# First feed-forward planes through two PSUM banks by thirds, and a fourth bank for the front ring

## The chip, the cores and the metric

The kernel runs on one core of a Trainium2 chip. Its engines work side by side and meet only at semaphores: TensorE (PE, whose weight loads are shown as PEld), VectorE (DVE), ScalarE (ACT), GpSimd (POOL) and SyncE (SP), which issues the DMAs. The metric is the device time of one execution in microseconds.

## The reference

The input x is 8 x 96 x 128 x 128 in float32. Two layers run one after the other. In short:

```
# layer 0
x = x + cluster(ln_c(x))            # 1x1 convolutions, 4 heads, 2x2 folds, 4 centres per fold:
                                    # cosine similarity, sigmoid, hard assignment to the best centre,
                                    # gather to the centres and back, 1x1 projection
t = tokens(x)
t = t + ffn(ln_t(t))                # h = relu(qlin(x, W1, b1)); y = qlin(h, W2, b2); 96 -> 384 -> 96
# layer 1
x = x + conv(ln_c(x))               # depthwise 3x3, 1x5, 5x1, then 1x1, times the normalised input
t = t + ffn(ln_t(t))
```

`qlin` rounds both factors to an 8-bit float (5 exponent, 2 mantissa bits) and the sums to a 16-bit one.

## The kernel before, in words

Three phases run one after the other. Phase A is layer 0 (and the normalisation that opens layer 1), phase B is the depthwise convolutions, phase C is the rest of layer 1. The change touches phase A alone.

Phase A treats 32 quarters of 64 x 64 tokens. A quarter has 4096 tokens: 8 chunks of 512, each held as 4 blocks of 128 tokens by 96 channels. The work of a quarter is spread over five steps: in step i the kernel runs the feed-forward network of quarter i, the projection back of quarter i+1 ("out", added to the tokens by DVE, "x1"), the similarities of quarter i+2, the centres of quarter i+3, and the turn of quarter i+4 from channels to tokens ("fwd"). A step has 9 slots, s = 0 to 8. Every engine has its own list, written out by hand, of what it does in each slot; an engine never leaves its order. The tables `BIG_AT`, `OUT_AT`, `FWD_AT`, `C_AT_BEFORE` and so on say in which slot each piece stands.

The feed-forward network of chunk k is: PE turns the 8-bit tokens to channels (`pe_q8`, L258); ACT copies them from PSUM to `q8c` (L296); PE multiplies by W1, three matmuls of 128 x 512, into the tile `hid`, which fills three PSUM banks (L272); ACT copies all three thirds with one instruction, 128 x 1536, to `h` (L307); DVE adds the bias and takes the maximum with zero in three instructions (L229) and rounds to 8 bits in one (L233), giving `hq`; PE multiplies by W2 (`pe_y`, L288); ACT copies the result (`y`, L318); DVE adds it to the tokens (L240, L244). In slot s, PE turns chunk s+1, runs the W1 product of chunk s and the W2 product of chunk s-1.

PSUM has eight banks. Phase A gives three to `hid`, two to the "back" ring (`bbank`: q8, y, and the turned planes "c" that ACT takes out by L805) and three to the "front" ring (`fbank`: all other products). A ring gives its banks round robin in program order, 36 uses of the front ring a step. Before PE writes a use it waits until the use that held the bank last has been read out:

```
n = self.number[stage, k]
for _ in self.uses:
    n -= len(self.banks)
```

In slots 3 to 6 the front ring's uses are, in order: big 6, big 7, out 0, out 1, pool; out 2, out 3, cf; out 4, out 5, simT 0, cn2; out 6, out 7, fwd 0, fwd 1. "big" is the product L608, taken out by ACT (L776, L777) and reduced by DVE (L902). "out" is L691, taken out by DVE (L983). "cn2" and its like are the tiny products at L682. "pabd" is the projection matrix that DVE writes in slot 2 (L976).

Of the kernel before, what the change touches and what calls it, by code (L numbers as in the profile page):

```python
# [53 lines left out]
class Events:  # L54
# [132 lines left out]
class FeedForward:  # L187
# [121 lines left out]
    def act_y(self, act, i, k):  # L309
# [61 lines left out]
def phase_a(nc, consts, x, wf_t, wf, bf, wv_t, bv, wp_t, bp, alpha, beta, w1, b1, w2, b2, gamma, beta_ln, x2_dram, x3_dram):  # L371
# [4 lines left out]
    with ExitStack() as ctx:  # L376
# [3 lines left out]
        for s in range(FFN_SLOTS):  # L380
# [17 lines left out]
            if s == AGG_AT:  # L398
# [172 lines left out]
        def _(pe):  # L571
# [182 lines left out]
        def _(act):  # L754
# [53 lines left out]
            def body(i):  # L808
                q1, q2, q3, q4, p = i + 1, i + 2, i + 3, i + 4, i - 1
                for s in range(FFN_SLOTS):  # L810
                    if i.real and s + 1 < NK:
                        ff.act_q8(act, i, s + 1)
                    if i.real and s < NK:
                        ff.act_hidden(act, i, s)
                    for k in C_AT_BEFORE.get(s, ()):
                        if p.real:
                            c_out(p, k)
                    for c in BIG_AT.get(s, ()):
                        if q2.real:
                            big(q2, c)  # L820
                    if i.real and s >= 1:
# [981 lines left out]
```

## Time and profile before

| | us |
|---|---|
| median of 3 runs | 4256.6 (4250.14 to 4260.43) |
| the profiled execution | 4258.63 |
| its span | 4256.8 |
| phase A in it | about the first 2142 |
| PE, DVE, ACT busy in the whole span | 3309.3, 3027.4, 2686.4 |

The span runs from the first to the last instruction. A busy time is the time in which an engine had an instruction in work. Idle time of an engine costs something only where its next work is on the path that sets the end. L12 is line 12 of the kernel. "A <- B" in a row of waits says that A's engine stood idle until B was done.

### The profile page before, as it was taken

Reading aid. Unit: us, or ns where it says so; the run is one execution under the profiler, and the core shown is the slowest. Engines: PE = TensorE matmul, PEld = TensorE weight load, DVE = VectorE, ACT = ScalarE, POOL = GpSimd, SP = SyncE. Lnnn points to the kernel's source line nnn. Section 1 sums busy time; section 2 is a strip of 40 time slices with the busy share of each in tenths; the row PEclk is TensorE's granted clock in tenths of the full one; section 3 lists DMA queues with packets and bytes.
Section 4 is the critical chain, followed back from the end, with each engine's and each line's share of the span. In section 5 each row is a group of like instructions: output and inputs, shape, how many; then the busy total and the mean of one; then the engine's idle time right before and its main releaser. Section 6 shows DMA issues by size and latency. Waiting matters only on the chain. (4 is left out here: it accounts for less than half of the span.)

```text
span 4256.8 us, 81198 instructions
## 1 busy us (share of the span) xinstructions
PE 3309.3 (78%) x26660; PEld 2549.8 (60%) x26660; DVE 3027.4 (71%) x7852; ACT 2686.4 (63%) x5250; POOL 1408.0 (33%) x1892
## 2 busy tenths in 40 slices
PE   6767777676776777767669999999788777778787
PEld 5556555555555555555549999999544444444443
DVE  4888888888888888888842222222388788778787
ACT  2567667676676776766752222222388788888887
POOL 3555555555555555555310000000022221212221
PEclk8888788888888887888879999999799999999998
DMA  3133232332323323222146656656766565666562
GB/s 62 44 75 83 67 77 61 75 83 68 75 65 78 83 61 75 71 72 68 53 111 163 168 160 164 166 161 165 183 178 179 151 178 156 174 170 171 155 175 77
DMA packets 733857, 489.89 MB, mean 115 GB/s; under 512 B 420796, under 2 KB 712956, under 8 KB 721276
## 3 DMA queue, kind: packets, MB, share of 16 engines
q1 hardware_dynamic: 733564, 486.32, 43.3%
q8 instruction: 143, 2.34, 0.2%
q14 instruction: 150, 1.23, 0.1%
HBM read 284.42 MB, written 201.33 MB: 114 GB/s over the span
## 5 line engine op out<-in xcount | busy, mean ns | idle before, releaser
L1722 POOL TENSOR_SCALAR C_var<-C_st 128x16 f32<-128x16 f32 x64 | 13.2, 207 | 1775.8 <-DVE C_st L178 1775.8
L1264 PE MATMUL B_ps_row<-B_g,B_z 128*128 128x128 f32 x4608 | 555.8, 277 | 0.6 <-ACT B_g L1296 0.6
L1264 PEld LDWEIGHTS B_ps_row<-B_g,B_z 128*128 128x128 f32 x4608 | 532.2, 193 | 0.7 <-ACT B_g L1296 0.7
L178 DVE BATCH_NORM_STATS2 A_st<-A_xT 128x6 f32<-128x192 f32 x1536 | 446.7, 350 | 30.7 <-ACT A_xT L764 17.3
L166 POOL TENSOR_TENSOR A_rstd<-A_var,A_expo 128x16 f32<-128x16 f32 x128 | 454.2, 3549 | 23.8 <-POOL A_var L163 23.6
L1357 DVE TENSOR_TENSOR B_mid<-B_ps_row,B_row_bias 128x512 f32<-128x512 f32 x192 | 132.8, 692 | 457.7 <-PE B_ps_row L1264 447.7
L1394 ACT ACTIVATE C_q<-C_xT,C_shift,C_rstd 128x96 fp8e5<-128x96 f32 x1024 | 392.0, 457 | 41.5 <-POOL C_shift L1729 41.0
L307 ACT ACTIVATE A_h<-A_hid 128x1536 f16<-128x1536 f32 x256 | 370.6, 1448 | 55.4 <-PE A_hid L272 51.6
L307 ACT ACTIVATE C_h<-C_hid 128x1536 f16<-128x1536 f32 x256 | 370.5, 1447 | 20.0 <-PE C_hid L272 12.9
L794 ACT ACTIVATE A_xc<-A_xT,A_shift,A_rstd 128x96 f32<-128x96 f32 x1024 | 379.4, 462 | 0.0
L229 DVE TENSOR_SCALAR A_hq<-A_h,A_b 128x512 f16<-128x512 f16 x768 | 240.8, 369 | 178.9 <-ACT A_h L307 178.6
L608 PE MATMUL A_fbank<-A_big_w,A_xq 97*128 97x112 f32 x2048 | 305.4, 313 | 66.3 <-DVE A_pabd L976 64.6
L608 PEld LDWEIGHTS A_fbank<-A_big_w,A_xq 97*128 97x128 f32 x2048 | 297.0, 227 | 93.6 <-DVE A_pabd L976 79.4
L1308 ACT ACTIVATE B_y<-B_ps_col,B_col_bias 128x512 f32<-128x512 f32 x192 | 132.0, 687 | 318.2 <-PE B_ps_col L1275 318.2
L1577 PE MATMUL C_fbank<-C_y3q,C_pw 96*96 96x512 f32 x512 | 280.9, 632 | 48.6 <-DVE C_gated L1653 24.3
L229 DVE TENSOR_SCALAR C_hq<-C_h,C_b 128x512 f16<-128x512 f16 x768 | 224.6, 349 | 122.9 <-ACT C_h L307 80.5
L288 PE MATMUL A_bbank<-A_w,A_hq 128*128 128x96 f16 x3072 | 219.4, 234 | 98.7 <-ACT A_x3h L805 85.8
L288 PEld LDWEIGHTS A_bbank<-A_w,A_hq 128*128 128x128 f16 x3072 | 197.7, 115 | 145.5 <-issue 112.7
L296 ACT ACTIVATE A_q8c<-A_bbank 96x512 bf16<-96x512 f32 x256 | 150.8, 590 | 197.5 <-PE A_bbank L258 196.2
L691 PE MATMUL A_fbank<-A_pabd,A_simT 128*128 128x384 f32 x512 | 261.2, 646 | 5.2 <-DVE A_xT L983 4.3
L1436 ACT ACTIVATE C_y<-C_bbank 96x512 f16<-96x512 f32 x256 | 150.2, 587 | 160.7 <-PE C_bbank L1423 156.9
L1586 PEld LDWEIGHTS C_fbank<-C_cst,C_gated 96*128 96x128 f32 x1024 | 113.2, 145 | 220.7 <-issue 111.9
(162 smaller groups left out, 7778.4 us busy)
## 6 DMA issues: line engine op xcount, KB each, us to landing
A_xq<-in_x SPq DMA_DIRECT2D x32, 1536.0 KB, 8.9
x_scratch<-A_xT SPq DMA_DIRECT2D x64, 768.0 KB, 3.2
x_scratch<-A_x3h SPq DMA_DIRECT2D x64, 768.0 KB, 5.4
B_z<-x_scratch SPq DMA_DIRECT2D x96, 512.0 KB, 5.0
y_scratch<-B_y SPq DMA_DIRECT2D x96, 512.0 KB, 3.7
C_x3q<-x_scratch SPq DMA_DIRECT2D x32, 1536.0 KB, 9.2
C_y3q<-y_scratch SPq DMA_DIRECT2D x32, 1536.0 KB, 15.5
C_xT<-x_scratch SPq DMA_DIRECT2D x64, 768.0 KB, 14.7
```

The lines of the kernel that those rows point to most:

```text
L166: m = pool.tensor_tensor(rstd[:, o:o + n], var[:], expo[:, 0:n], ALU.pow)
L178: return dve.bn_stats(st[:, n:n + 2, :].rearrange("p t s -> p (t s)"), x[:, n * C:(n + 2) * C].rearrange("p (t c) -> p c t", t=2))
L229: r = dve.tensor_scalar(self.hq[:, b, s], self.h16[:, b, s], self.w["b1"][:, j:j + 1], 0.0, ALU.add, ALU.max)
L288: m = pe.matmul(bank[:, t * C:(t + 1) * C], self.hq[:, b, s:s + P], self.w["w2"][:, j, :], start=(j == 0), stop=(j == NJ - 1))
L296: act.activation(self.q8c[:, k % 2, :], self.ring.bank("q8", k)[0:C, 0:CH], ACT.Copy).then_inc(self.ev["q8c"], 1)
L307: act.activation(self.h16[:, k % 2, :], self.hid[:, :], ACT.Copy).then_inc(ev["h16"], 1)
L608: m = pe.matmul(bank[:, t * BIGN:(t + 1) * BIGN], xq[q.buf(NX)][:, n * P:(n + 1) * P], big_w[:, :], start=True, stop=True)
L691: pe.matmul(front.bank("out", k)[:, 0:CW], simT[q.buf(2)][:, k, :], pabd[:], start=True, stop=True).then_inc(ev["out_full"], 1)
L794: m = act.activation(xc3[:, k // 4, t % (NT // 2), :], xT[u.buf(NB)][:, t * C:(t + 1) * C], ACT.Identity, scale=rstd3[:, t:t + 1], bias=sh ...
L1264: m = pe.matmul(ps_row[h][:, b * P:(b + 1) * P], z[c.buf(NB)][:, h * HB + b, d:d + W], g[c.buf(2)][:, d, :], start=(d == 0), stop=(d == 2))
L1394: m = act.activation(self.q8[:, t, :], x[:, t * C:(t + 1) * C], ACT.Identity, scale=self.rstd[:, t:t + 1], bias=self.shift[:, t:t + 1], sa ...
L1577: pe.matmul(rows(front.bank("pw", k)[0:C, 0:CH]), pw[:], group(y3q[q.buf(2)], k), start=True, stop=True).then_inc(ev["pw_full"], 1)
```

## The change

The class of the feed-forward network gets a variant for phase A. `hid` becomes two tiles of one bank each, and the thirds n = 3k+j of all chunks alternate between them. Each third has its own matmul with its own semaphore step, its own ACT copy (three of 128 x 512 in place of one of 128 x 1536), and its own wait on DVE. PE writes third n when ACT has copied third n-2. The first two thirds of a chunk stay where all three stood; the last third is moved back: on PE and ACT behind the first "big" of the slot, or, in slots without a "big", behind the turned planes (and, on PE, behind the W2 product of the chunk before). The bank that `hid` gives up makes the front ring four banks long.

```diff
+        self.hid2 = [ctx.enter_context(nc.psum_tensor(phase + f"hid{p}", [P, CH], F32)) for p in range(2)]
...
+    def pe_hidden(self, pe, i, k, j):
+        ev, n = self.ev, NJ * k + j
+        if j == 0:
+            pe.wait_ge(ev["q8c"], ev.at("q8c", i, k))
+        if n >= 2:
+            pe.wait_ge(ev["h16"], ev.at("h16", i, n - 2))
...
+        pe.matmul(self.hid2[n % 2][:], self.w["w1"][:, j * P:(j + 1) * P], self.q8c[:, k % 2, :],
+                  start=True, stop=True).then_inc(ev["hidden"], 1)
+    def act_hidden(self, act, i, k, j):
...
+        act.activation(self.h16[:, k % 2, j * CH:(j + 1) * CH], self.hid2[n % 2][:], ACT.Copy).then_inc(ev["h16"], 1)
+    def dve_hidden(self, dve, i, k):
+        ev, b = self.ev, k % 2
+        for j in range(NJ):
+            s = slice(j * CH, (j + 1) * CH)
+            dve.wait_ge(ev["h16"], ev.at("h16", i, NJ * k + j))
+            r = dve.tensor_scalar(self.hq[:, b, s], self.h16[:, b, s], self.w["b1"][:, j:j + 1], 0.0, ALU.add, ALU.max)
...
-        front = Ring(front_uses, [ctx.enter_context(nc.psum_tensor(f"A_fbank{p}", [P, 512], F32)) for p in range(3)])
+        front = Ring(front_uses, [ctx.enter_context(nc.psum_tensor(f"A_fbank{p}", [P, 512], F32)) for p in range(4)])
...
-                        ff.pe_hidden(pe, i, s)
+                        ff.pe_hidden(pe, i, s, 0)
+                        ff.pe_hidden(pe, i, s, 1)
                     for k in C_AT_BEFORE.get(s, ()):
                         if p.real:
                             c_turn(i, p, k)
-                    for c in BIG_AT.get(s, ()):
-                        if q2.real:
-                            big(i, c)
-                    if i.real and s >= 1:
+                    bigs = BIG_AT.get(s, ()) if q2.real else ()
+                    for c in bigs[:1]:
+                        big(i, c)
+                    if i.real and s >= 1 and not bigs:
+                        ff.pe_y(pe, i, s - 1)
+                    if i.real and s < NK:
+                        ff.pe_hidden(pe, i, s, 2)
+                    for c in bigs[1:]:
+                        big(i, c)
+                    if i.real and s >= 1 and bigs:
                         ff.pe_y(pe, i, s - 1)
```

ACT's list is cut in the same way; there `y` stays last in every slot.

PE, end of slot 5 and start of slot 6 of a step in the middle of phase A, before. L691 is out 4 and 5, L620 simT 0, the tiny L682 cn2, L258 the turn of chunk 7, L272 the W1 product of chunk 6, L288 the W2 product of chunk 5.

```order
L691 MATMUL A_fbank<-A_pabd,A_simT 128x384 [waits A_x1] x2
L620 MATMUL A_fbank<-A_cst,A_sim 128x128 [waits A_cfc,A_sim]
L620 MATMUL A_fbank<-A_cst,A_sim 128x128 x3
L682 MATMUL A_fbank<-A_csq,A_cst 96x4 [waits A_x1,A_csq]
L258 MATMUL A_bbank<-A_idb,A_q 96x128 [waits A_norm2,A_cout]
L258 MATMUL A_bbank<-A_idb,A_q 96x128 x3
L272 MATMUL A_hid<-A_q8c,A_w 128x512 [waits A_h16,A_q8c]
L272 MATMUL A_hid<-A_q8c,A_w 128x512 x2
L288 MATMUL A_bbank<-A_w,A_hq 128x96 [waits A_y16,A_hq]
```

The same place now; L746 is out, L675 simT, L737 cn2, L348 a third of the W1 product.

```order
L746 MATMUL A_fbank<-A_pabd,A_simT 128x384 [waits A_pooled]
L746 MATMUL A_fbank<-A_pabd,A_simT 128x384 [waits A_x1]
L675 MATMUL A_fbank<-A_cst,A_sim 128x128 [waits A_x1,A_sim]
L675 MATMUL A_fbank<-A_cst,A_sim 128x128 x3
L737 MATMUL A_fbank<-A_csq,A_cst 96x4 [waits A_cfc,A_csq]
L258 MATMUL A_bbank<-A_idb,A_q 96x128 [waits A_norm2,A_cout]
L258 MATMUL A_bbank<-A_idb,A_q 96x128 x3
L348 MATMUL A_hid<-A_q8c,A_w 128x512 [waits A_h16,A_q8c]
L348 MATMUL A_hid<-A_q8c,A_w 128x512 [waits A_h16]
L288 MATMUL A_bbank<-A_w,A_hq 128x96 [waits A_y16,A_hq]
L288 MATMUL A_bbank<-A_w,A_hq 128x96 x11
L348 MATMUL A_hid<-A_q8c,A_w 128x512 [waits A_h16]
```

The order of the front ring is the same; what cn2 waits for has moved from an `x1` of DVE (out 4 read out) to `cfc` (cf read out, a slot earlier). The last third stands behind the W2 product.

PE, slot 3, before: the W1 product of chunk 3, big 6, big 7 and the W2 product of chunk 2.

```order
L272 MATMUL A_hid<-A_q8c,A_w 128x512 [waits A_h16,A_q8c]
L272 MATMUL A_hid<-A_q8c,A_w 128x512 x2
L608 MATMUL A_fbank<-A_big_w,A_xq 128x112 [waits A_pabd]
L608 MATMUL A_fbank<-A_big_w,A_xq 128x112 x3
L608 MATMUL A_fbank<-A_big_w,A_xq 128x112 [waits A_sided]
L608 MATMUL A_fbank<-A_big_w,A_xq 128x112 x3
L288 MATMUL A_bbank<-A_w,A_hq 128x96 [waits A_y16,A_hq]
```

The same place now; L663 is big.

```order
L348 MATMUL A_hid<-A_q8c,A_w 128x512 [waits A_h16,A_q8c]
L348 MATMUL A_hid<-A_q8c,A_w 128x512 [waits A_h16]
L663 MATMUL A_fbank<-A_big_w,A_xq 128x112 [waits A_big]
L663 MATMUL A_fbank<-A_big_w,A_xq 128x112 x3
L348 MATMUL A_hid<-A_q8c,A_w 128x512 [waits A_h16]
L663 MATMUL A_fbank<-A_big_w,A_xq 128x112 [waits A_pabd]
L663 MATMUL A_fbank<-A_big_w,A_xq 128x112 x3
L288 MATMUL A_bbank<-A_w,A_hq 128x96 [waits A_y16,A_hq]
```

The wait for `pabd` has moved from big 6 to big 7.

ACT, slot 4, before: q8c of chunk 5, h of chunk 4, two turned planes, y of chunk 3.

```order
L296 ACTIVATE A_q8c<-A_bbank 96x512 [waits A_q8_full]
L307 ACTIVATE A_h<-A_hid 128x1536 [waits A_relu,A_hidden]
L805 ACTIVATE A_x3h<-A_bbank,A_gb 96x512 [waits A_x3_st1,A_c_full]
L805 ACTIVATE A_x3h<-A_bbank,A_gb 96x512 [waits A_c_full]
L318 ACTIVATE A_y<-A_bbank 128x384 [waits A_yb,A_y_full]
```

The same place now; L361 is a third of h, L867 a turned plane.

```order
L296 ACTIVATE A_q8c<-A_bbank 96x512 [waits A_q8_full]
L361 ACTIVATE A_h<-A_hid 128x512 [waits A_relu,A_hidden]
L361 ACTIVATE A_h<-A_hid 128x512 [waits A_hidden]
L867 ACTIVATE A_x3h<-A_bbank,A_gb 96x512 [waits A_x3_st1,A_c_full]
L867 ACTIVATE A_x3h<-A_bbank,A_gb 96x512 [waits A_c_full]
L361 ACTIVATE A_h<-A_hid 128x512 [waits A_hidden]
L318 ACTIVATE A_y<-A_bbank 128x384 [waits A_yb,A_y_full]
```

The last third of h now follows the two turned planes.

## Rows read from the trace of the kernel before

**Rows 1.** Busy time by engine, of phase A and of the rest.

```profile
core 0: us, PE busy (x) PEld busy (x) DVE busy (x) ACT busy (x) POOL busy (x), PEclk, DMA share, GB/s
0.00:2142.00 2142.00, 1516.17 (x14228) 1197.86 (x14228) 1770.81 (x4819) 1434.73 (x2984) 1161.67 (x1624) 0.83 0.29 70
2142.00:4257.00 2115.00, 1793.16 (x12432) 1351.99 (x12432) 1256.60 (x3034) 1251.68 (x2267) 246.35 (x268) 0.95 0.59 161
```

**Rows 2.** Who waited for whom, 300 to 1900 us: total, times, longest.

```profile
DVE A_hq L229 <- ACT A_h L307: 137.6, 94, 3.0
PE A_fbank L682 <- DVE A_xT L983: 85.9, 25, 3.9
PE A_fbank L608 <- DVE A_pabd L976: 49.2, 24, 2.6
DVE A_n L902 <- ACT A_dots L777: 29.2, 54, 1.2
DVE A_y16b L240 <- ACT A_y L318: 10.6, 24, 0.8
```

**Rows 3.** Timeline of DVE, slot 0 of two steps: start, length, instruction.

```profile
988.25 0.88 DVE L229 TENSOR_SCALAR A_hq<-A_h,A_b 128x512 f16<-128x512 f16 x3
...
1054.64 0.87 DVE L229 TENSOR_SCALAR A_hq<-A_h,A_b 128x512 f16<-128x512 f16 x3
```

**Rows 4.** Timeline of all engines, end of slot 5 and slot 6.

```profile
1026.01 1.00 DVE L983 TENSOR_TENSOR A_xT<-A_fbank,A_xT 128x384 f32<-128x384 f32 x2
...
1026.70 0.45 PE L682 MATMUL A_fbank<-A_csq,A_cst 96*96 96x4 f32 x2 [3.89 <-DVE A_xT L983]
...
1027.68 0.59 ACT L296 ACTIVATE A_q8c<-A_bbank 96x512 bf16<-96x512 f32 x1 [3.67 <-PE A_bbank L258]
...
1027.99 0.14 DVE L1027 TENSOR_SCALAR A_cn<-A_fbank 96x4 f32<-96x4 f32 x1
...
1028.96 1.45 ACT L307 ACTIVATE A_h<-A_hid 128x1536 f16<-128x1536 f32 x1 [0.69 <-PE A_hid L272]
...
1030.45 0.88 DVE L229 TENSOR_SCALAR A_hq<-A_h,A_b 128x512 f16<-128x512 f16 x3 [2.32 <-ACT A_h L307]
```

**Rows 5.** Timeline of all engines, slots 2 and 3.

```profile
1002.37 1.30 DVE L976 TENSOR_SCALAR A_pabd<-A_fbank,A_rden 32x96 f32<-32x96 f32 x4
...
1003.72 3.45 PE L608 MATMUL A_fbank<-A_big_w,A_xq 97*128 97x112 f32 x16 [2.60 <-DVE A_pabd L976]
...
1006.97 1.17 PE L288 MATMUL A_bbank<-A_w,A_hq 128*128 128x96 f16 x12
...
1007.85 0.55 DVE L902 TENSOR_REDUCE A_n<-A_sq 128x16 f32<-128x384 f32 x1 [1.15 <-ACT A_dots L777]
...
1008.17 0.49 ACT L318 ACTIVATE A_y<-A_bbank 128x384 f16<-128x384 f32 x1 [0.35 <-PE A_bbank L288]
...
1008.56 2.96 ACT L794 ACTIVATE A_xc<-A_xT,A_shift,A_rstd 128x96 f32<-128x96 f32 x8
```

**Rows 6.** Timeline of all engines, slot 4.

```profile
1011.42 0.58 ACT L851 ACTIVATE A_sim<-A_dots,A_ab 128x256 f32<-128x256 f32 x1
...
1011.91 0.57 ACT L296 ACTIVATE A_q8c<-A_bbank 96x512 bf16<-96x512 f32 x1
...
1013.72 1.43 ACT L805 ACTIVATE A_x3h<-A_bbank,A_gb 96x512 f32<-96x512 f32 x2
1013.86 1.00 DVE L229 TENSOR_SCALAR A_hq<-A_h,A_b 128x512 f16<-128x512 f16 x3 [1.29 <-ACT A_h L307]
...
1014.63 0.67 PE L288 MATMUL A_bbank<-A_w,A_hq 128*128 128x96 f16 x12 [1.39 <-ACT A_x3h L805]
...
1014.89 0.72 DVE L233 TENSOR_SCALAR A_hq<-A_hq 128x1536 uint16<-128x1536 uint16 x1
```

**Rows 7.** Timeline of all engines, slot 1 of the next step.

```profile
1058.24 3.17 PE L608 MATMUL A_fbank<-A_big_w,A_xq 97*128 97x112 f32 x16
1058.44 1.45 ACT L307 ACTIVATE A_h<-A_hid 128x1536 f16<-128x1536 f32 x1
1059.79 0.48 ACT L776 ACTIVATE A_sq<-A_fbank 128x384 f32<-128x384 f32 x1
1059.93 0.88 DVE L229 TENSOR_SCALAR A_hq<-A_h,A_b 128x512 f16<-128x512 f16 x3 [2.16 <-ACT A_h L307]
```

**Rows 8.** Groups by line and shape, 0 to 2140 us: busy, mean ns.

```profile
L307 ACT ACTIVATE A_h<-A_hid 128x1536 f16<-128x1536 f32 x248 | 359.0, 1447 | 53.0 <-PE A_hid L272 49.4
...
L318 ACT ACTIVATE A_y<-A_bbank 128x384 f16<-128x384 f32 x248 | 123.3, 497 | 37.1 <-PE A_bbank L288 37.0
```

More of the change, by code:

```diff
@@ L318, in act_y, with __init__ @@
         act.activation(self.y16[:, k % 2, :], self.ring.bank("y", k)[:, 0:CW], ACT.Copy).then_inc(ev["y16"], 1)
+class SplitFeedForward(FeedForward):
+    def __init__(self, nc, ctx, phase, ev, ring, xT, wts, idb):
+        self.nc, self.ev, self.ring, self.xT, self.w, self.idb = nc, ev, ring, xT, wts, idb
+        sb = lambda n, s, d: ctx.enter_context(nc.sbuf_tensor(phase + n, s, d))
+        self.hid2 = [ctx.enter_context(nc.psum_tensor(phase + f"hid{p}", [P, CH], F32)) for p in range(2)]
+        self.xc = sb("xc", [P, NT // 2, C], F32)
+        self.q8 = sb("q8", [P, NT, C], FP8)
+        self.q8c = sb("q8c", [C, 2, CH], BF16)
+        self.h16 = sb("h16", [P, 2, NJ * CH], F16)
+        self.hq = sb("hq", [P, 2, NJ * CH], F16)
+        self.y16 = sb("y16", [P, 2, CW], F16)
+        self.y16b = sb("y16b", [P, 2, CW], F16)
+        self.st = sb("st2", [P, NT, 3], F32)
+        self.rstd = sb("rstd2", [P, NT], F32)
+    def pe_hidden(self, pe, i, k, j):
[4 more added lines that the diff above has]
+            pe.wait_ge(ev["h16"], ev.at("h16", i, n - 2))
+        elif begun(i - 1):
+            pe.wait_ge(ev["h16"], ev.at("h16", i - 1, NJ * NK - 2 + n))
+        pe.matmul(self.hid2[n % 2][:], self.w["w1"][:, j * P:(j + 1) * P], self.q8c[:, k % 2, :],
+                  start=True, stop=True).then_inc(ev["hidden"], 1)
+    def act_hidden(self, act, i, k, j):
+        ev, n = self.ev, NJ * k + j
+        act.wait_ge(ev["hidden"], ev.at("hidden", i, n))
+        if j == 0:
+            if k >= 2:
+                act.wait_ge(ev["relu"], ev.at("relu", i, k - 2))
+            elif begun(i - 1):
+                act.wait_ge(ev["relu"], ev.at("relu", i - 1, NK - 2 + k))
+        act.activation(self.h16[:, k % 2, j * CH:(j + 1) * CH], self.hid2[n % 2][:], ACT.Copy).then_inc(ev["h16"], 1)
[5 more added lines that the diff above has]
+            r = dve.tensor_scalar(self.hq[:, b, s], self.h16[:, b, s], self.w["b1"][:, j:j + 1], 0.0, ALU.add, ALU.max)
+        r.then_inc(ev["relu"], 1)
+        dve.wait_ge(ev["relu"], ev.at("relu", i, k))
+        u = self.hq[:, b, :].bitcast(U16)
+        dve.tensor_scalar(u, u, ROUND8, ROUND8, ALU.add, ALU.subtract).then_inc(ev["hq"], 1)
@@ L405, in phase_a @@
         NSQ = 4
-        ev = Events(nc, ctx, "A_", dict(FFN_EVENTS,
+        ev = Events(nc, ctx, "A_", dict(FFN_EVENTS, hidden=NJ * NK, h16=NJ * NK,
                     xT=NK, bn1=NK, ln1=2, ln1_s=4, pooled=1, cf=1, cfc=1, csq=1, cn2=1, cn2c=1, cpow=1, chat=1,
@@ L484, in phase_a @@
         s_val, s_pa = front.bank("val", 0)[0:C + 1, 0:HM], front.bank("pa", 0)[:, 0:C + 1]
-        ff = FeedForward(nc, ctx, "A_", ev, back, xT, wts, idb)
+        ff = SplitFeedForward(nc, ctx, "A_", ev, back, xT, wts, idb)
         HR = QS // 2
@@ L813, in body @@
                     if i.real and s < NK:
-                        ff.act_hidden(act, i, s)
+                        ff.act_hidden(act, i, s, 0)
+                        ff.act_hidden(act, i, s, 1)
                     for k in C_AT_BEFORE.get(s, ()):
@@ L817, in body @@
                             c_out(p, k)
-                    for c in BIG_AT.get(s, ()):
-                        if q2.real:
-                            big(q2, c)
+                    bigs = BIG_AT.get(s, ()) if q2.real else ()
+                    for c in bigs[:1]:
+                        big(q2, c)
+                    if i.real and s < NK:
+                        ff.act_hidden(act, i, s, 2)
+                    for c in bigs[1:]:
+                        big(q2, c)
                     if i.real and s >= 1:
```

## The prediction

> **What bounds the kernel now.** I read first the busy times by stretch [rows 1]. Phase A takes 2142 us and the rest 2115. The change touches phase A alone, so the 2115 us stay. In phase A no engine is full: DVE is busy 1770.8 us (83%), PE 71%, ACT 67%, POOL 54%. A phase in which the busiest engine reaches 83% is bound by round trips between engines that keep a fixed order. The reader should look for the waits of the busiest engine, since each microsecond that DVE stops standing idle can shorten the step, while idle time of the others matters only where DVE waits behind it.
>
> A step lasts 1054.64 - 988.25 = 66.4 us [rows 3], so the 1600 us of the table of waits hold 24 steps. In them DVE waited 137.6 us for `h`, 29.2 for the "big" copies and 10.6 for `y` [rows 2]: 5.7, 1.2 and 0.4 us a step. The timeline then says where in the step the 5.7 us stand: 2.16 in slot 1 [rows 7], 1.29 in slot 4 [rows 6], and the rest, 5.7 - 2.16 - 1.29 = 2.3, in slot 6, where one step shows 2.32 [rows 4]. Each of the three has its own cause.
>
> Slot 6 is a bank's doing. PE stood 3.89 us before the tiny cn2 product until DVE had read out 4 by L983 at about 1026.5. Only then could it turn chunk 7; ACT, idle 3.67 us, copied q8c at 1027.68 and h at 1028.96 to 1030.41; DVE, which had nothing left after 1027.99 + 0.14 = 1028.13, started at 1030.45 [rows 4]. This PE wait came 25 times in 24 steps, 3.4 us each [rows 2]. Slot 3 is the same in small: PE stood 2.60 us before big 6 until `pabd` was written, and DVE then waited for the copies of big, 1.15 us for the second [rows 5].
>
> Slot 1 and slot 4 are no bank's doing. In slot 1 the chain sum, values, q8, q8c, h starts at DVE itself. In slot 4 ACT comes late: it copies y (to 1008.66), then normalises for 2.96 us, then the sigmoid, q8c and h [rows 5, 6].
>
> **The change part by part.**
>
> *Fourth bank, slot 6.* cn2 now waits for cf, read out in slot 4. simT has to wait as before for DVE's similarity, and cn2 follows at once. PE's 3.89 us go, and q8, q8c and h come some 3.9 us sooner, before the 1028.13 at which DVE is ready: 1030.41 - 3.9 = 1026.5. The last third stands behind the W2 product of chunk 5 (up to 1.17 us [rows 5]) and takes one more copy of 0.6, which ends near 1027.5, still before DVE needs it. So the DVE wait of 2.2 to 2.3 us goes whole. The last three steps have no cn2; with the first ones that fill the pipeline I count 28 steps: 28 x 2.2 = -62 us. Next late there is DVE's own work. Bounds: 0 (another engine is as late) and 2.3 x 31 = -71.
>
> *Price of the split on ACT.* From 497 ns for 384 columns and 1447 for 1536 [rows 8] a column costs 950/1152 = 0.825 ns, and a copy of 512 columns 497 + 128 x 0.825 = 603 ns. Two copies of the planes took 1.43 us back to back [rows 6], 0.7 each. Three thirds then take between 1.6 and 1.8 us where one copy took 1.45: +0.15 to +0.36 a slot, 8 x 31 slots, 37 to 90 us of ACT time in all. ACT has 707 us idle in phase A [rows 1], so this costs only where DVE stands behind h, in slots 1 and 4, and is counted there.
>
> The trace gives copies a fixed part of 497 - 384 x 0.825 = 180 ns [rows 8]. The Trainium skill ("ScalarE: Activation LUTs", What ACT_TABLE_LOAD costs) states 186 ns + 0.833 N with an overlap of about 93 ns between neighbours. By that page two more instructions cost 0.19 us a slot, near the low end of the range.
>
> *Slot 1.* Before, DVE starts at 1059.93 and needs 0.88 us plus the rounding. Now the first two thirds come at 1058.44 + 0.6 and + 1.1; then ACT does the first big (its L776 and L777, 0.7 us with overlap), and then the last third, 0.6. Its big has to be there: PE takes half of 3.17 = 1.6 us for it from about 1058.0, to 1059.7 [rows 7]. So the last third ends at about 1060.9 to 1061.0 against 1059.9 for the whole of h, and DVE then has only one third left (0.35) where it had 0.88. Net +0.45 us a step: 31 x 0.45 = +14. Bounds: 0 (PE at its faster clock, big early) and +1.0.
>
> *Slot 0.* The last third stands there behind two turned planes (1.43) and a big (0.7). ACT had h 1.0 us ahead of DVE, and with PE and ACT no longer held by the front ring in slots 5 to 8 they run ahead of DVE by more. I take 0; if that cover is gone it costs 0.6 a step.
>
> *Slots 3 and 4.* big 6 no longer waits for `pabd`; big 7 does. It starts at 1003.7 and takes 1.7, so the W2 product stands at 1005.5 to 1006.6 in place of 1006.97 to 1008.14, and y is copied by 1007.1 in place of 1008.66 [rows 5]. DVE loses its waits for big, 1.2 us a step [rows 2]. But then slot 4: ACT ends its 2.96 us at 1010.1, sigmoid 1010.6, q8c 1011.2, two thirds 1012.3, two planes 1013.7. PE can run the W2 product of chunk 3 (0.67 [rows 6]) only when the first plane has been copied, and the last third only after it; so the last third is copied from about 1013.9 to 1014.6, DVE finishes it by 1014.9, and the rounding by 1015.4. Before, the rounding ended at 1014.89 + 0.72 = 1015.61 [rows 6]. The gain of slot 3 is thus nearly eaten by the moved third: -0.2, and -0.3 because y now lies before the rounding's end and L240 needs no wait (0.4 a step [rows 2]). Together -0.5 x 31 = -16. Bounds: -1.6 (third in time) and +1.4 (planes and third one after the other with nothing gained in slot 3).
>
> Sum: -62 + 14 + 0 - 16 = -64 us. Against the profiled execution, 4258.6 - 64 = 4194.6. The median of the runs is 2 us lower, which gives 4192.6; I say 4192.
>
> **The rivals.**
>
> *A. The moved third costs more than the bank brings.* The place is ACT: the last third behind planes and big in slots 0, 1, 4. Price by the upper bounds: 0.6 + 1.0 + 1.4 = 3.0 us a step, 93 us in all. With the 62 of slot 6 still gained it ends 31 us above, near 4288. It decides once the DVE waits for `h` in these slots grow by more than 2.2 us a step. For it: in slots 1 and 4 DVE already waits behind exactly this copy. Against it: two thirds of DVE's work move ahead of the wait, which gives 0.5 us back each time.
>
> For A the Trainium skill ("Perfetto Trace Analysis", Optimizing Scalar/DVE Operations) holds one half of a rule, that larger operations pay where the engine is saturated, and the other half speaks for the change: where ScalarE only causes bubbles elsewhere, smaller pieces finish the work sooner. ACT at 67% [rows 1] is the second case.
>
> *B. The slot 6 wait is only handed on.* PE is released 3.9 us earlier, yet DVE then meets another late piece in slots 7 to 0, such as a bank, POOL's power (its rows were not on the path before) or ACT's 3 us of normalising. A third of the gain stays, -20, with +14 from slot 1: about 4250. For it: every engine of the step keeps a fixed order, with waits under 0.5 us close by. Against it: in slots 7 and 8 DVE shows next to no waits now.
>
> *C. The thirds are in time everywhere.* With PE and ACT free of the bank waits, slot 1 costs nothing and the waits of slots 3 and 4 (1.2 + 1.29 + 0.4 = 2.9) go too: -(2.2 x 28 + 2.9 x 31) = -152, near 4105. Against it: slot 4's path through the first plane and the W2 product is longer than before.
>
> **How the numbers follow.** The forecast has 0.63, A 0.12, B 0.14, C 0.11. A measurement of this kernel can tell a difference of 0.2%, 8.5 us, from none. Faster by more than that: the forecast, C, and half of B, 0.81. Within it: the other half of B, 0.07. Slower: A, 0.12. The forecast's own range, by the bounds, is 4150 to 4235. The stated range reaches into C and over B, 4130 to 4250; A and the far end of C are left out.
>
> **What would show it.** In the new profile the wait of the cn2 product for L983's successor is gone (under 0.3 us a step) and with it DVE's wait for h in slot 6. big 6 starts with no wait, big 7 waits for `pabd`. DVE's waits for thirds of h stand in slots 1 and 4, before the last third, of 1.5 to 2.5 us. The step lasts 64.2 to 64.6 us. ACT's busy time in phase A grows by 60 to 100 us (own durations), PE's and DVE's do not. The stretch behind phase A still takes 2115 us. The prediction is wrong if the step does not fall below 66, if DVE waits for a last third in slot 0 or in slot 6, or if a new PE wait of over 2 us stands in slots 5 to 8.

## The result

| | before | after |
|---|---|---|
| median, us | 4258.52 (4 runs, 4250.14 to 4263.05) | 4211.52 (4 runs, 4210.19 to 4213.31) |
| profiled execution, its span | 4258.63, 4256.8 | 4210.19, 4208.4 |

The ratio of after to before is 0.9892, with a 95% interval of 0.9875 to 0.9909. The change made the kernel faster by 47 us; the forecast was 4192, for a gain of 64. The time lies in the stated range and the direction was right, but a quarter of the gain did not come.

The time fell in phase A. L216 is a DVE instruction that runs twice for each of the 32 quarters. The trace's row on it gives the shortest, median and longest duration in ns and the first and last start; first of before, then of after:

```profile
L216 DVE TENSOR_TENSOR A_xc<-A_xT,A_st x64: 1728/1744/1760, 121.8 to 2144.9; 128x1536 f32<-128x1536 f32 x64
```

```profile
L216 DVE TENSOR_TENSOR A_xc<-A_xT,A_st x64: 1728/1744/1760, 116.9 to 2100.5; 128x1536 f32<-128x1536 f32 x64
```

The last start came 44.4 us sooner, 4.9 of them already gained at the first. The other 39.5 make 1.27 us for each of the 31 steps between, where about 2 were forecast (64 us). The span fell by 48.4 us, so 8.9 of them lie outside these steps, where the forecast had no term. Busy times of after, by stretch, against [rows 1]:

```profile
core 0: us, PE busy (x) PEld busy (x) DVE busy (x) ACT busy (x) POOL busy (x), PEclk, DMA share, GB/s
0.00:2095.00 2095.00, 1512.19 (x14221) 1187.11 (x14222) 1759.01 (x4816) 1454.44 (x3473) 1165.26 (x1624) 0.81 0.29 71
2095.00:4209.00 2114.00, 1795.74 (x12442) 1353.40 (x12440) 1258.96 (x3037) 1254.26 (x2289) 247.76 (x269) 0.95 0.59 161
```

DVE's share went from 83% to 84%, and the granted clock of phase A fell from 0.83 to 0.81. The waits of after from 300 to 1900 us (total, times, longest), against [rows 2]:

```profile
DVE A_hq L369 <- ACT A_h L361: 151.8, 124, 2.2
...
PE A_fbank L703 <- DVE A_summed L1028: 85.8, 25, 3.4
...
PE A_fbank L746 <- DVE A_xT L1050: 27.5, 24, 1.3
...
DVE A_aT L1033 <- PE A_fbank L703: 14.9, 25, 0.6
...
DVE A_n L969 <- ACT A_dots L839: 5.0, 25, 0.2
```

In 24.7 steps of 64.9 us DVE waited 6.1 us a step for h, where [rows 2] had 5.7. The wait for the big copies fell from 1.2 to 0.2, and that for y is gone. One more row has to be read: PE stood 3.4 us a step for `summed` at the start of slot 1. Before, the row of that wait was this:

```profile
PE A_fbank L648 <- DVE A_summed L961: 38.2, 24, 2.1
```

That is 1.6 us a step. Part of the time that PE got free elsewhere was spent standing here.

Slot 6 of after, all engines, against [rows 4]:

```profile
1065.17 0.66 PE L675 MATMUL A_fbank<-A_cst,A_sim 128*128 128x128 f32 x4
...
1065.66 0.26 PE L737 MATMUL A_fbank<-A_csq,A_cst 96*96 96x4 f32 x2
...
1067.42 1.06 ACT L361 ACTIVATE A_h<-A_hid 128x512 f16<-128x512 f32 x2
...
1068.65 0.60 ACT L361 ACTIVATE A_h<-A_hid 128x512 f16<-128x512 f32 x1 [0.17 <-PE A_hid L348]
...
1071.26 0.14 DVE L1094 TENSOR_SCALAR A_cn<-A_fbank 96x4 f32<-96x4 f32 x1
1071.32 0.86 DVE L369 TENSOR_SCALAR A_hq<-A_h,A_b 128x512 f16<-128x512 f16 x3
```

cn2 follows simT with no wait in this step, the last third of h is there at 1069.25, and DVE passes from L1094 to L369 without a pause, 2 us later. This part came as written.

Slot 1 of after, all engines, against [rows 7]:

```profile
1032.77 0.51 PE L703 MATMUL A_fbank<-A_summed,A_wv_ext 97*97 97x16 f32 x2 [3.43 <-DVE A_summed L1028]
...
1034.41 1.89 PE L663 MATMUL A_fbank<-A_big_w,A_xq 97*128 97x112 f32 x8
...
1034.91 0.84 DVE L369 TENSOR_SCALAR A_hq<-A_h,A_b 128x512 f16<-128x512 f16 x2 [1.37 <-ACT A_h L361]
...
1036.33 0.49 ACT L838 ACTIVATE A_sq<-A_fbank 128x384 f32<-128x384 f32 x1 [0.97 <-PE A_fbank L663]
...
1036.82 0.60 ACT L361 ACTIVATE A_h<-A_hid 128x512 f16<-128x512 f32 x1
...
1037.46 0.36 DVE L369 TENSOR_SCALAR A_hq<-A_h,A_b 128x512 f16<-128x512 f16 x1 [1.71 <-ACT A_h L361]
```

DVE waits twice, 1.37 + 1.71 = 3.08 us, where it waited 2.16 in the step of [rows 7]. The big took 1.89 us, and ACT stood 0.97 us for it before it could come to the last third. Slot 4 of after, against [rows 6]:

```profile
1055.03 1.43 ACT L867 ACTIVATE A_x3h<-A_bbank,A_gb 96x512 f32<-96x512 f32 x2
...
1055.94 1.12 PE L288 MATMUL A_bbank<-A_w,A_hq 128*128 128x96 f16 x12 [0.87 <-ACT A_x3h L867]
...
1056.85 0.63 PE L348 MATMUL A_hid<-A_q8c,A_w 96*128 96x512 bf16 x1
...
1057.52 0.60 ACT L361 ACTIVATE A_h<-A_hid 128x512 f16<-128x512 f32 x1 [1.06 <-PE A_hid L348]
```

Here the moved third runs plane, W2 product, third, one after the other. DVE's next row is its last third at 1058.15, after a wait of 2.16 us.

### The profile page after: what moved, and what is told of

It reads as the page before. It is cut to its first block and busy times, and to the rows that moved or that the text cites. A ratio compares the mean times of both kernels' runs of the same rounds, so it can differ in the third digit from the quotient of the medians.

```text
span 4208.4 us, 81710 instructions
## 1 busy us (share of the span) xinstructions
PE 3307.9 (79%) x26660; PEld 2540.5 (60%) x26660; DVE 3018.0 (72%) x7852; ACT 2708.7 (64%) x5762; POOL 1413.0 (34%) x1892
## 5 line engine op out<-in xcount | busy, mean ns | idle before, releaser
L361 ACT ACTIVATE A_h<-A_hid 128x512 f16<-128x512 f32 x768 | 426.7, 592 | 66.8 <-PE A_hid L348 63.2
L178 DVE BATCH_NORM_STATS2 A_st<-A_xT 128x6 f32<-128x192 f32 x1536 | 442.9, 349 | 24.7 <-ACT A_xT L826 11.5
L369 DVE TENSOR_SCALAR A_hq<-A_h,A_b 128x512 f16<-128x512 f16 x768 | 250.1, 363 | 198.5 <-ACT A_h L361 193.5
L663 PEld LDWEIGHTS A_fbank<-A_big_w,A_xq 97*128 97x128 f32 x2048 | 337.2, 237 | 63.4 <-DVE A_big_w L1098 29.7
L663 PE MATMUL A_fbank<-A_big_w,A_xq 97*128 97x112 f32 x2048 | 333.9, 319 | 23.4 <-DVE A_big_w L1098 21.9
L348 PE MATMUL A_hid<-A_q8c,A_w 96*128 96x512 bf16 x768 | 313.4, 467 | 31.5 <-ACT A_h L361 29.5
L288 PE MATMUL A_bbank<-A_w,A_hq 128*128 128x96 f16 x3072 | 219.0, 235 | 121.5 <-DVE A_hq L373 73.5
L288 PEld LDWEIGHTS A_bbank<-A_w,A_hq 128*128 128x128 f16 x3072 | 189.2, 114 | 188.0 <-DVE A_hq L373 119.2
L746 PE MATMUL A_fbank<-A_pabd,A_simT 128*128 128x384 f32 x512 | 234.6, 588 | 35.5 <-DVE A_xT L1050 35.5
```

The costliest lines, as they stand in the source:

```text
L178: return dve.bn_stats(st[:, n:n + 2, :].rearrange("p t s -> p (t s)"), x[:, n * C:(n + 2) * C].rearrange("p (t c) -> p c t", t=2))
L288: m = pe.matmul(bank[:, t * C:(t + 1) * C], self.hq[:, b, s:s + P], self.w["w2"][:, j, :], start=(j == 0), stop=(j == NJ - 1))
L348: pe.matmul(self.hid2[n % 2][:], self.w["w1"][:, j * P:(j + 1) * P], self.q8c[:, k % 2, :], start=True, stop=True).then_inc(ev["hidden"], 1)
L361: act.activation(self.h16[:, k % 2, j * CH:(j + 1) * CH], self.hid2[n % 2][:], ACT.Copy).then_inc(ev["h16"], 1)
L663: m = pe.matmul(bank[:, t * BIGN:(t + 1) * BIGN], xq[q.buf(NX)][:, n * P:(n + 1) * P], big_w[:, :], start=True, stop=True)
```

## The experiments

Theory: the fourth front bank gives back DVE's waits in slots 6 and 3, and the moved third costs part of it in slots 1, 2 and 4. Rivals: the cut into thirds is itself the gain; any further bank would do. All ratios are against the kernel before, timed on the same chip; the change itself stands at 0.9892. Differences in us between two versions are between their medians. The versions were timed at different times, and the kernel before that belongs to each ratio lies between 4250 and 4259, so such a difference is good to some 8 us.

**One part at a time**

*Front ring back to three banks, the thirds as changed.*

```diff
-        front = Ring(front_uses, [... for p in range(4)])
+        front = Ring(front_uses, [... for p in range(3)])
```

> The changed kernel with its front ring of three banks in place of four (one PSUM bank stays unused); the thirds and their places as changed. Theory (the fourth bank brings the gain, the moved thirds cost part of it): the wait of PE before the cn2 product (3 to 4 us a step) and the wait before big for pabd come back; DVE again waits 1.5 to 2.5 us for h in slot 6 and keeps its waits for the moved thirds in slots 1, 2 and 4. Step 66.5 to 68 us, time 4260 to 4310. Rival (the thirds themselves bring the gain, by letting DVE start before the whole of h is there): 4205 to 4230, as the changed kernel.

Measured: 4307.2, ratio 1.0129 (1.0112 to 1.0146), 95 us above the change. Its waits, 300 to 1900 us:

```profile
DVE A_hq L369 <- ACT A_h L361: 199.0, 179, 2.2
...
PE A_fbank L737 <- DVE A_xT L1050: 93.5, 24, 4.0
```

The cn2 wait is back, 3.9 us each. So the cut, the move and `hid` in two banks lose 53 us by themselves, and the fourth front bank brings 95. The gain of 47 is the difference of two larger numbers.

*The bank given to the back ring in place of the front ring.*

```diff
-        front = ... range(4)
-        back = ... range(2)
+        front = ... range(3)
+        back = ... range(3)
```

> The changed kernel with the freed bank given to the back ring (q8, y, planes: three banks) and the front ring left at three. Theory (the worth of the bank is in the front ring's waits for DVE's L983, pabd and ACT's copies): those waits stay; the W2 product of slots 4 and 5 and the last third behind it no longer wait for the first plane, which gives back at most 1 us in slot 4; time 4270 to 4310. Rival (any further bank would do, PE is short of banks everywhere): 4210 to 4240.

Measured: 4283.9, ratio 1.0077 (1.0051 to 1.0104). PE still stood 91.6 us for L1050 before cn2. The bank has to be in the front ring; in the back ring it gives 23 of the 95 us, and that number is rough, since this version's seven runs spread from 4262 to 4303.

*Before, with ACT's copy cut into three and a wait of DVE for each third, nothing moved.*

```diff
-        act.activation(self.h16[:, k % 2, :], self.hid[:, :], ACT.Copy).then_inc(ev["h16"], 1)
+        n = ev.per["h16"] // NK
+        for j in range(n):
+            s = slice(j * (NJ // n) * CH, (j + 1) * (NJ // n) * CH)
+            act.activation(self.h16[:, k % 2, s], self.hid[:, s], ACT.Copy).then_inc(ev["h16"], 1)
```

Here n is 3.

> The kernel before (three banks for hid, three for the front ring, nothing moved) with ACT's copy of h cut into three, one behind the other, and DVE waiting for each third. Theory: the copies take 0.15 to 0.36 us longer a slot, and DVE starts 0.85 us sooner where it waits, so its rounding ends 0.2 us sooner to 0.1 later in slots 1, 4 and 6: time 4235 to 4262, within 0.5% of before. Rival (the split by itself is what made the change faster): 4215 to 4230. Rival (ACT's added fixed cost is on the path): above 4270.

Measured: 4240.1, ratio 0.9962 (0.9951 to 0.9974). DVE's wait for h fell from 137.6 to 63.3 us, that for y rose from 10.6 to 24.7. So the cut alone gains 14 us and is not what loses in the first run; there the loss must lie in giving up `hid`'s third bank and in the move, which no run takes apart.

**The place of the last third**

*Last third at once behind the first two, in all slots.*

```diff
                         ff.pe_hidden(pe, i, s, 1)
+                        if s in range(NK):
+                            ff.pe_hidden(pe, i, s, 2)
```

(and the same on ACT; the later place goes).

> The changed kernel with the last third of h at once behind the first two, in all slots, on PE and ACT. Theory: DVE's wait for the last third in slot 4 (2.15 us) falls to under 1 and that of slot 2 (0.7) goes; in slot 1 the last third comes about 1.2 us sooner, but PE has to stand until ACT has copied the first third, so the bigs come 1.2 later and DVE waits for them instead. Step 62.8 to 64, time 4150 to 4185. Rival (the place of the third is of no account, since DVE then waits for something else): 4205 to 4220. Second rival (PE standing in its list for ACT's copy costs more than the place brings): 4220 to 4260.

Measured: 4283.8, ratio 1.0078 (1.0062 to 1.0095), 72 us above the change: the second rival, and stronger than written. Its waits:

```profile
PE A_hid L348 <- ACT A_h L361: 189.6, 191, 2.7
...
DVE A_n L973 <- ACT A_dots L841: 76.5, 104, 1.2
DVE A_hq L369 <- ACT A_h L361: 74.1, 130, 1.4
```

With two banks PE can write the third only when ACT has read the first, and it stands 7.9 us a step for that. DVE waits less for h but 3.2 us a step for bigs. The move that I had booked as a cost is what makes two banks bearable in slots 0 to 3.

*The same in slots 4 to 7 alone.*

```diff
+                        if s in (4, 5, 6, 7):
+                            ff.pe_hidden(pe, i, s, 2)
```

> The changed kernel with the last third at once behind the first two in slots 4 to 7 only (those without a big). Theory: the 2.15 us wait of slot 4 goes nearly whole, the planes come 0.6 us later on ACT, which nobody waits for: step 63 to 63.8, time 4165 to 4185. Rival (a wait of the same length appears for y or the planes): 4205 to 4215.

Measured: 4205.1, ratio 0.9892 (0.9876 to 0.9909), within 0.2% of the change. The wait of 2.15 us for the last third went and this one came in the same slot:

```profile
1053.36 1.12 PE L288 MATMUL A_bbank<-A_w,A_hq 128*128 128x96 f16 x12
1054.51 0.49 ACT L318 ACTIVATE A_y<-A_bbank 128x384 f16<-128x384 f32 x1 [0.45 <-PE A_bbank L288]
1055.03 0.36 DVE L240 TENSOR_TENSOR A_y16b<-A_y,A_b 128x384 f16<-128x384 f16 x1 [1.52 <-ACT A_y L318]
```

DVE now waits for y, whose W2 product stands behind the planes. The rival was right: in slot 4 ACT's late start costs DVE, whatever is put first.

**The clock in slot 1**

*14 matmuls without use, in the bank of the values product, while PE stands for `summed`.*

```diff
+                bank_free(front, i, "val", 0)
+                for _ in range(14):
+                    pe.matmul(front.bank("val", 0)[:, 0:HID], wts["w1"][:, 0:P], wts["w1"][:, :], start=True, stop=True)
                 pe.wait_ge(ev["summed"], ev.at("summed", q, 0))
-                bank_free(front, i, "val", 0)
```

> The changed kernel with 14 matmuls of 96x384 bf16 without use, written to the bank of the values product while PE would stand 3.4 us for DVE's summed at the start of slot 1; nothing else is added. Theory (of DVE's 3.1 us wait in slot 1 a part is PE's lower clock after the long stand: the first big there took 1.89 us, the like in slot 0 1.04 to 1.15): with PE busy the big of slot 1 takes 1.04 to 1.1, the last third comes 1 to 1.3 us sooner, DVE's wait before it falls from 1.7 to about 0.6; step 63.5 to 64, time 4165 to 4190. Rival (the wait in slot 1 is the order and the semaphores, and the clock does not matter): 4205 to 4220. If the fillers run past the moment at which summed is there: above 4215.

Measured: 4110.7, ratio 0.9673 (0.9656 to 0.9691). It is 101 us under the change by the medians, some 93 by the ratios, and either is at least twice what the theory gave. Stretches of one step, slot 0, slots 1 and 2, slots 3 and 4, first of the change:

```profile
core 0: us, PE busy (x) PEld busy (x) DVE busy (x) ACT busy (x) POOL busy (x), PEclk, DMA share, GB/s
1026.60:1032.70 6.10, 2.52 (x21) 2.39 (x21) 5.93 (x11) 2.57 (x7) 5.77 (x2) 0.84 0.67 154
1032.70:1045.00 12.30, 12.23 (x128) 11.12 (x132) 7.28 (x21) 8.47 (x22) 8.04 (x17) 0.66 0.01 2
1045.00:1057.00 12.00, 8.40 (x93) 6.55 (x83) 10.35 (x32) 11.46 (x30) 4.35 (x14) 0.90 0.59 114
```

then with the fillers:

```profile
core 0: us, PE busy (x) PEld busy (x) DVE busy (x) ACT busy (x) POOL busy (x), PEclk, DMA share, GB/s
978.70:984.70 6.00, 4.80 (x35) 3.61 (x35) 5.83 (x11) 2.50 (x7) 5.72 (x2) 1.00 0.70 151
984.70:997.00 12.30, 11.11 (x156) 9.61 (x156) 9.54 (x29) 11.55 (x32) 8.81 (x20) 1.00 0.02 4
997.00:1009.00 12.00, 8.78 (x73) 6.38 (x73) 9.94 (x30) 10.22 (x25) 4.50 (x14) 1.00 0.68 132
```

The column before the last two is the granted clock. After the stand of 3.43 us the change ran slots 1 and 2 at a mean of 0.66, mostly at 1.2 GHz, and PE was busy 12.23 of 12.30 us there. With the fillers the same stretches ran at 1.00, 2.4 GHz. The low clock is not new with the change. The kernel before had it too, in the step of [rows 7]:

```profile
core 0: us, PE busy (x) PEld busy (x) DVE busy (x) ACT busy (x) POOL busy (x), PEclk, DMA share, GB/s
1057.00:1069.00 12.00, 11.84 (x140) 10.71 (x140) 7.96 (x23) 8.59 (x19) 8.33 (x19) 0.72 0.23 49
```

But there it came in some steps only. Over the 12.3 us behind the values product the clock was 1.00 in 12 of the 24 steps between 300 and 1900 us, 0.86 in 2 and 0.72 or 0.73 in 10. In the changed kernel it was 0.66 or 0.67 in all 25, each behind a stand of 3.43 or 3.44 us. In slot 1, behind the fillers (L703), the big took 1.04 us in place of 1.89:

```profile
981.23 2.44 PE L703 MATMUL A_fbank<-A_w 96*128 96x384 bf16 x14
...
985.68 1.04 PE L663 MATMUL A_fbank<-A_big_w,A_xq 97*128 97x112 f32 x8
...
986.56 0.84 DVE L369 TENSOR_SCALAR A_hq<-A_h,A_b 128x512 f16<-128x512 f16 x2 [1.14 <-ACT A_h L361]
988.03 0.35 DVE L369 TENSOR_SCALAR A_hq<-A_h,A_b 128x512 f16<-128x512 f16 x1 [0.63 <-ACT A_h L361]
```

DVE waited 1.14 + 0.63 = 1.77 us in place of 3.08, and the 0.72 and 0.23 us of slots 2 and 3 are gone. That is 2.3 of the 3.6 us by which the step shown fell (64.9 to 61.3); the table in the next part has the means by slot.

*6 of the same matmuls in the kernel before.*

```diff
+                bank_free(front, i, "val", 0)
+                for _ in range(6):
+                    pe.matmul(front.bank("val", 0)[:, 0:HID], wts["w1"][:, 0:P], wts["w1"][:, :], start=True, stop=True)
                 pe.wait_ge(ev["summed"], ev.at("summed", q, 0))
-                bank_free(front, i, "val", 0)
```

> The kernel before with 6 of the matmuls without use (96x384 bf16) in the bank of the values product while PE stands 1.6 to 2.1 us for summed at the start of slot 1. Theory (PE's lower clock after a long stand costs the changed kernel more than the one before, because the fourth bank made that stand 3.4 us long and the moved third put a big on the path of h): here the fillers bring less, 10 to 40 us: 4215 to 4245. Rival (the clock is a cost of its own that both kernels carry alike): the full 100 us that the fillers gave the changed kernel, 4150 to 4170. None at all: 4250 to 4260.

Measured: 4243.6, ratio 0.9976 (0.9966 to 0.9986), 11 us under before. The clock of its phase A (300 to 1900 us) was 0.85. The fillers did their work: in all 24 steps the clock behind the values product was now 0.98 to 1.00. That it pays so little fits the steps of the kernel before itself. Those with a clock of 0.98 to 1.00 behind aT lasted 66.1 us in the mean, those with 0.72 to 0.75 66.2: what slots 1 to 3 lost by the low clock, slot 4 gave back. So filling that stand pays 11 us before the change and about 100 after it, as the theory said. The number of fillers differs, since the stand does.

**Moves in the lists**

*The values product behind the thirds of slot 1.* PE's list held the turn of chunk 2 and the W1 product of chunk 1 behind a wait that neither needs.

```diff
-                    if q1.real and s == VAL_AT:
-                        values(i)
                     if i.real and s + 1 < NK:
                         ff.pe_q8(pe, i, i, s + 1)
...
+                        if s in (VAL_AT,):
+                            ff.pe_hidden(pe, i, s, 2)
+                    if q1.real and s == VAL_AT:
+                        values(i)
```

(and the last third of slot 1 in the same place on ACT; its later place goes).

> The changed kernel with the values product on PE behind the q8 turn and all three thirds of slot 1 (the last third stands with the first two in slot 1 alone, on PE and ACT). Theory (PE stands 3.4 us for DVE's summed with the turn of chunk 2 and the W1 product of chunk 1 behind it in its list, which need nothing of it): h of slot 1 is there when DVE comes, the 1.37 and 1.71 us go, aT keeps its 0.6; step 61.5 to 62.5, time 4110 to 4150. Rival (ACT or PE is as late by another way, so that the wait goes to slot 2, to the bigs or to y): 4180 to 4215.

Measured: 4116.7, ratio 0.9685 (0.9669 to 0.9701), 95 us under the change, inside the theory's range. In its waits h is down to a third, and about 1.3 us a step for the bigs came in its place:

```profile
DVE A_hq L369 <- ACT A_h L361: 44.4, 42, 2.1
...
DVE A_n L973 <- ACT A_dots L841: 33.3, 40, 1.2
```

*ACT's normalisation of chunks 6 and 7 one slot later.*

```diff
-NORM3_AT, NORM3_LATE = {7: (0, 1), 8: (2, 3)}, {2: (4, 5), 3: (6, 7)}
+NORM3_AT, NORM3_LATE = {7: (0, 1), 8: (2, 3)}, {2: (4, 5), 4: (6, 7)}
```

> The changed kernel with ACT's normalisation of chunks 6 and 7 (2.96 us) in slot 4 behind y in place of slot 3. Theory (slot 4's wait of 2.15 us stands because ACT comes late: 2.96 us of normalising, the sigmoid, q8c, two thirds, two planes, last third): q8c and h come near 3 us sooner there, the 2.15 us go, and slot 5's h has cover of some 6 us; step 62.7 to 63.3, time 4145 to 4170. Rival (the wait hangs on the order first plane, W2 product, last third on PE, not on when ACT starts): 4200 to 4215.

Measured: 4155.5, ratio 0.9774 (0.9758 to 0.9790), 56 us under the change. Slot 4's wait hangs on when ACT starts, as the theory said.

*Both moves.*

```diff
+                    if q1.real and s == VAL_AT:
+                        values(i)
...
+NORM3_AT, NORM3_LATE = {7: (0, 1), 8: (2, 3)}, {2: (4, 5), 4: (6, 7)}
```

> The changed kernel with both moves, the values product behind all three thirds of slot 1 and the normalisation of chunks 6 and 7 in slot 4. Theory (the two waits are apart): 4060 to 4085, step about 60; the distance to the kernel before with the same two moves is 70 to 110 us, larger than the 47 of the change, since the waits that the moved third added are gone. Rival (the fourth bank is worth the same 47 us or less there): 4100 to 4125.

Measured: 4115.0, ratio 0.9667 (0.9645 to 0.9690). That is no more than the first move alone: the rival. Of its waits:

```profile
DVE A_n L973 <- ACT A_dots L841: 49.6, 52, 1.2
PE A_fbank L703 <- DVE A_summed L1032: 39.8, 26, 1.6
DVE A_hq L369 <- ACT A_h L361: 28.4, 42, 1.3
```

h costs 1.1 us a step and the bigs 1.9. Its phase A clock was 0.85, that of the first move alone 0.88. In one step of it the two bigs of slot 1 took 3.25 us together after a stand of 1.34, and DVE waited 1.15 for the second. I take the clock to have eaten the second move, and the steps bear this out. In the mean slot 4 was 1.6 us shorter than with the first move alone, and slot 2 was 1.4 longer. Over the 12.3 us behind the values product the clock had been 0.86 in every step; now it was 0.72 in most, and the one step in which it was 0.86 lasted 60.0 us, the one before it 61.3.

*Both moves and 6 fillers.*

```diff
+                bank_free(front, i, "val", 0)
+                for _ in range(6):
+                    pe.matmul(front.bank("val", 0)[:, 0:HID], wts["w1"][:, 0:P], wts["w1"][:, :], start=True, stop=True)
                 pe.wait_ge(ev["summed"], ev.at("summed", q, 0))
-                bank_free(front, i, "val", 0)
```

> The same with 6 fillers before the values product. Theory (PE still stands about 1.6 us there and does the two bigs of slot 1 in 2.8 us in place of 2.0, and DVE waits 1.1 us for the second): 20 to 35 us under val_norm3, 4030 to 4060. Rival (the clock is up by now, the fillers only delay the values product): within 8 us of val_norm3 or above it.

Measured: 4095.8, ratio 0.9618 (0.9598 to 0.9637), 19 us under the run without fillers, a microsecond short of what was expected of them, and well above the 4030 to 4060 of the theory, since the run that it starts from had missed its own. It is the fastest version here. But the clock of its phase A was still 0.86 and DVE still waited for bigs, so the fillers did not restore the clock as they did in the kernel without the moves. Behind the values product it was 1.00 in only 2 of the 25 steps between 300 and 1800 us, which lasted 59.8 and 59.9 us, and 0.72 in most others, which lasted 61.3 to 61.6. The mean step, 61.2 us, is 0.1 under that without fillers; most of what the profiled execution gained lies in the first and last steps of the phase. Why the clock stayed low is open.

*Both moves in the kernel before.*

```diff
-                    if q1.real and s == VAL_AT:
-                        values(i)
...
                         ff.pe_hidden(pe, i, s)
+                    if q1.real and s == VAL_AT:
+                        values(i)
```

(with the table of the normalisation as above).

> The kernel before (three banks for hid, three in front) with the values product behind the turn and the W1 product of slot 1, and ACT's normalisation of chunks 6 and 7 moved from slot 3 to slot 4. Theory (these two waits of DVE, 2.16 and 1.29 us, stand in both kernels and hang on no bank): step down by 2.5 to 3.5 us, time 4145 to 4180. Rival (without the fourth bank PE is late everywhere and nothing is gained): 4235 to 4260.

Measured: 4142.7, ratio 0.9728 (0.9708 to 0.9747). Two lists changed in the old kernel gain 112 us, more than twice the change. Between the two kernels with both moves lie 28 us; I had expected 70 to 110. It would be wrong to conclude that the fourth bank was worth less here. In slot 6 it still did its work: DVE stood idle 1.9 us a step there without it and 0.1 with it. But in slot 2 the kernel with four banks and thirds stood idle 2.9 us a step and this one 0.2, and the clock behind the values product was mostly 0.72 there and 1.00 in nearly every step here. The two steps of the version with fillers whose clock was 1.00 took 59.8 and 59.9 us, against 62.2 in the mean here. By my estimate from these, 2.3 us in 31 steps, the distance would be about 70 us at the full clock. No run shows that as a time.

## Why the prediction came out as it did

The table gives the mean length of each slot on DVE in us, over the 23 to 25 steps that begin between 300 and 1840 us. A slot ends with the end of the rounding of its chunk; slot 1 begins with the end of aT.

| slot | before | after | after, 14 fillers | forecast | measured |
|---|---|---|---|---|---|
| 1 | 3.85 | 4.88 | 3.55 | +0.45 | +1.03 |
| 2 | 4.99 | 5.50 | 4.41 | none | +0.51 |
| 3 to 5 | 24.03 | 23.72 | 22.88 | -0.5 | -0.31 |
| 6 | 6.87 | 5.01 | 5.01 | -2.2 | -1.86 |
| 7, 8, 0, to aT | 26.36 | 25.74 | 25.56 | 0 | -0.62 |
| sum | 66.10 | 64.85 | 61.41 | -2.25 | -1.25 |

So a step in the middle of the phase gained little more than half of what was forecast. That three quarters of the 64 us came is in part luck: a gain of 0.62 us in slots for which nothing was forecast, and the 8.9 us outside the steps.

*What bounds the kernel.* Right: the round trips, and DVE's waits as the measure. Per step the waits of DVE for h, the bigs, aT and y went from 7.8 to 7.0 us (188.4 us in 24.2 steps, 171.7 in 24.7). The rest of the 1.25 us is in smaller pauses and in DVE's busy time, 56.0 to 55.7 us a step.

*Fourth bank, slot 6 (-62).* Right in mechanism, somewhat too large in size. The 2.32 us of [rows 4] are gone, and the run with three banks brings PE's wait and the time back. But that row was one of the longer ones. The forecast took the mean of all waits for h less one step's values for slots 1 and 4; over the steps the wait for h in slot 6 was 1.76 us, and the slot got shorter by 1.86.

*Price of the split.* A third took 592 ns in the mean (603 forecast), 426.7 us for all 768 against 370.6 for the 256 whole copies. That is 0.22 us a slot, inside the bounds of 0.15 to 0.36. The forecast's 60 to 100 us were by own durations, and so they came: 768 x 0.592 against 256 x 1.448 is 84 us more. But neighbours overlap: the group's busy time grew by 56, and ACT's whole busy time in phase A by 20.

*Slot 1 (+14).* This is the term that failed. From the end of aT to the end of the rounding DVE took 3.64 us in the step of [rows 7] (1057.76 to 1061.40) and 4.88 after (1033.53 to 1038.41); in the mean it took 3.85 before and 4.88 after. That is +1.03 us a step where I took +0.45 and named +1.0 as the upper bound, 18 us more in 31 steps. I had read PE's big at 1.6 us and did not ask how long PE would stand in front of it once it was released everywhere else. The stand grew from 1.6 to 3.4 us (2.2 in the version with three front banks), and the big took 1.89 us in every step. The run with 14 fillers shows the cause: the clock was at 1.00 there, and slot 1 took 3.55 us, less than before the change. So at the full clock the order of the last third costs nothing in slot 1; it is at the low clock that DVE waits long for the third behind the big.

*Slots 2 and 3.* DVE waited 0.72 and 0.23 us there for the third behind the big. I had no term for it, and in slot 2 it cost +0.51 us a step, 16 us in all. Both waits went with the fillers, so they are the same clock.

*Slot 0 (0).* Right: no wait for a third there.

*Slots 3 and 4 (-16).* Near in size. The bigs' wait fell by 1.0 us, y's 0.4 went, slot 4's wait for h rose from 1.29 to 2.16: -0.5 a step by these rows, and -0.31 by the table. That nothing in slot 4 but ACT's start matters, I had half seen: I listed ACT's chain, and then blamed the W2 product in front of the third. Taking it away moved the wait to y.

*The signs and the range.* Of the signs, the step was missed: 64.9 us in place of 64.2 to 64.6. I had also started from one step of 66.4 us, where the mean was 66.1. Big 7 was to wait for `pabd` and did not; no such row is left. The others came: cn2's wait is gone, there is no wait for a last third in slots 0 and 6, and the stretch behind phase A takes 2114 us. The range of 4150 to 4235, said to follow by the bounds, does not: their lower ends alone, -71, 0 and -1.6 x 31, lead to about 4136. It was narrower than the working allowed, and the time fell into it all the same.

*The rivals.* A (the moved third costs more than the bank brings) did not happen, and its reason came out the other way: with two banks a third that is not moved costs 72 us. On the page cited with A, the Trainium skill ("Perfetto Trace Analysis", Optimizing Scalar/DVE Operations): the second half of its rule, smaller pieces where ScalarE is not saturated, agrees with the cut alone in the kernel before (-14 us). B (the wait handed on) happened in part, at a place that I had not named: handed from DVE's wait in slot 6 to PE's stand before slot 1, and from there through the clock back to DVE.

## What to carry to other kernels

When a change frees an engine early, ask where in its fixed list it will stand next, for how long, and what it does right after: on TensorE the work behind a longer stand may run at half the clock, and a shorter wait elsewhere can be paid back there (here 3.43 us of standing, then a clock of 0.66). A wait in a hand-written list holds back all that is behind it; before adding a bank, look whether the instruction that waits, or long work in front of what others wait for, can simply stand later (here two such moves were worth 112 us in the old kernel, the whole change 47). And a cut into pieces over fewer banks has to be priced with its place: with the last piece right behind the others in all slots the kernel was 72 us slower than with it moved back.

## What was not expected of the hardware

After a stand of 3.43 us the granted clock over the next 12.3 us was 0.66 in the mean; with 2.44 us of that stand filled with matmuls it was 1.00, and stayed there in the 12 us after that. In the kernel before, the same place is seen both ways: after 1.59 us of standing two bigs took 1.94 us, while in the step of [rows 7], after 2.10 us, they took 3.17.

```profile
991.24 0.34 PE L648 MATMUL A_fbank<-A_summed,A_wv_ext 97*97 97x16 f32 x2 [1.59 <-DVE A_summed L961]
...
992.33 1.94 PE L608 MATMUL A_fbank<-A_big_w,A_xq 97*128 97x112 f32 x16
```

The length of the stand alone does not settle it: of 16 stands of 1.59 us in the kernel before, 10 were followed by a clock of 1.00, one by 0.86 and 5 by 0.72 or 0.73. What else decides is not shown. Fourteen matmuls of no use made the whole kernel more than 2% faster than the change without them.
